# First attention layer: ScalarE instead of VectorE copies the linear logits, one place behind the newest piece

## What is computed

```python
xl = (x @ Wl).reshape(n_nodes, heads, ch)
xr = (x @ Wr).reshape(n_nodes, heads, ch)
m = xl[src] + xr[dst]
e = leaky_relu(m, 0.2)
logits = einsum('ehc,hc->eh', e, att)
ex = exp(logits - segment_max(logits, dst)[dst])
alpha = ex / segment_sum(ex, dst)[dst]
out = segment_sum(alpha[:, :, None] * xl[src], dst)
```

## Time and profile before

| | us |
|---|---|
| median of 3 runs | 4667.72 |
| lowest, highest | 4667.09, 4673.2 |
| the profiled execution | 4674.29 |
| its span | 4672.5 |
| PE, DVE, ACT, POOL busy in the span | 3182.7, 3001.3, 1859.1, 3206.7 |
| DVE, ACT busy from 2400 to 3380 us (980 us) | 948.1, 883.9 |

### The profile page before, as it was taken

How to read it: one execution, slowest core, us unless ns; L and a number is a source line. 1 busy time by engine, 2 the same in 40 slices (tenths; PEclk the granted TensorE clock), 3 DMA queues, 4 the chain that set the end, 5 groups by cost and what they waited for, 6 DMA issues and landing times. The chain is left out here.

```text
span 4672.5 us, 94838 instructions
## 1 busy us (share of the span) xinstructions
PE 3182.7 (68%) x15556; PEld 2384.7 (51%) x15557; DVE 3001.3 (64%) x8993; ACT 1859.1 (40%) x6063; POOL 3206.7 (69%) x3436
## 2 busy tenths in 40 slices
PE   4666666666556566565678777777765888888882
PEld 3544444445344444443356666666533666666662
DVE  6545455454333333333689999999955887787776
ACT  3222222223000000000469899998842444444444
POOL 4777777775777777776177777777525777777772
PEclk7788888888777877877889999999987999999996
DMA  4666666665333333334377777777624877887874
GB/s 149 194 190 191 191 191 191 191 192 151 109 105 104 104 104 104 104 104 104 96 202 232 228 225 224 228 226 224 187 76 135 231 223 225 225 228 223 229 222 123
DMA packets 469973, 816.08 MB, mean 175 GB/s; under 512 B 86369, under 2 KB 271578, under 8 KB 469786
## 3 DMA queue, kind: packets, MB, share of 16 engines
q0 software_dynamic: 156464, 429.23, 33.9%
q1 hardware_dynamic: 246010, 294.61, 21.0%
q10 hardware_dynamic: 67312, 90.51, 5.4%
HBM read 640.60 MB, written 173.40 MB: 174 GB/s over the span
## 5 line engine op out<-in xcount | busy, mean ns | idle before, releaser
L1009 POOL DMA_INDIRECT rows<-table_d,idx x3224 | 3068.9, 952 | 997.2 <-issue 918.1
L1185 PE MATMUL psum<-rows,selw 128*128 x3648 | 1206.7, 491 | 803.4 <-POOLq L1025 720.0
L1185 PEld LDWEIGHTS psum<-rows,selw 128*128 128x128 f32 x3648 | 855.0, 245 | 1080.7 <-issue 935.5
L2065 ACT ACTIVATE px<-rows,px 128x64 f32 (+1 forms) x4480 | 1265.9, 367 | 105.5 <-ACT px L2056 101.9
L2130 PE MATMUL psum<-px,ohf 128*128 128x264 f32 (+1 forms) x3648 | 949.5, 405 | 66.4 <-ACT px L2065 63.1
L1157 DVE TENSOR_TENSOR acc<-acc,psum 125x256 f32 x456 | 191.3, 419 | 1013.2 <-PE psum L1185 1012.6
L2130 PEld LDWEIGHTS psum<-px,ohf 128*128 128x128 f32 x3648 | 678.4, 196 | 202.5 <-issue 45.3
L2081 PE MATMUL psum<-xr,ohT 125*128 x5472 | 706.6, 281 | 60.3 <-DMA ohT<-ohT_d 35.0
L1897 DVE TENSOR_TENSOR m<-rows,psum 128x1024 f32<-128x1024 f32 x456 | 553.8, 1214 | 236.4 <-POOLq L1025 150.3
L2081 PEld LDWEIGHTS psum<-xr,ohT 125*128 125x128 bf16 x5472 | 541.9, 100 | 201.8 <-issue 75.1
L1146 DVE TENSOR_SCALAR selw<-iotaw,dst_t,w_t 128x128 f32 x1824 | 517.7, 359 | 180.5 <-issue 126.4
(11 more groups left out here) (319 smaller groups left out, 2038.2 us busy)
## 6 DMA issues: line engine op xcount, KB each, us to landing
ohf<-oh_d SPq DMA_DIRECT2D x456, 256.0 KB
oh_d<-ohfk ACTq DMA_DIRECT2D x228, 256.0 KB, 2.8
ohT<-ohT_d SPq DMA_DIRECT2D x456, 128.0 KB
rows<-table_d,idx POOLq DMA_INDIRECT x3224, 2.7
part_d<-part SPq DMA_DIRECT2D x228, 132.0 KB
part_d<-part SPq DMA_DIRECT2D x228, 129.0 KB
ohT_d<-ohTk ACTq DMA_DIRECT2D x228, 128.0 KB
flg<-flags_d SPq DMA_DIRECT2D x228, 40.0 KB
```

Source lines behind the costliest of these rows:

```text
L1009: pool.indirect_dma_start(out=rows[0:n, s % RING, k, :], out_offset=None, in_=table, in_offset=bass.IndirectOffsetOnAxis(ap=idx[0:n, s // ...
L1185: last = nc.tensor.matmul(ps[g.pos % DEEP], sel[:, g.pos % DEEP, k, :], rows[:, bass.ds(r, 1), k, :].squeeze(1), start=k == 0, stop=k == K ...
L2065: last = nc.scalar.activation(px[:, i, k, h, 0:C], rows[:, bass.ds(r, 1), k, h * C:(h + 1) * C].squeeze(1), ACT.Copy, scale=px[:, i, k, h, ...
```

## The change

In the first attention layer (H > 1) `linear` leaves VectorE's list. ScalarE gets a stage `linear_logits` with lag 1, between `exps` and `take`. It waits for the block's landing by itself, copies the same numbers into the same place and counts the same semaphore. The second layer (H == 1) keeps VectorE's stage.

```diff
                                   (1, scale), *([(1, reduce)] if H > 1 else []), (2, take_ends), (0, add), (5, factor_line), (3, pick),
-                                  (0, linear), (3, before), (1, scan), (12, bring), (2, join), (3, after),
+                                  *([(0, linear)] if H == 1 else []), (3, before), (1, scan), (12, bring), (2, join), (3, after),
@@
-                    packed_pieces(act, mybir.EngineType.Activation, blocks3, 3, 10, (10, probs), (10, weigh), (3, exps), (4, take))
+
+                    def linear_logits(g):
+                        if g.place == 0:
+                            wait(act, s_turned, g.chunks(2))
+                        b, r = block_of(g), ring_of(g)
+                        wait_alone(act, s_landed, b + 1)
+                        nc.scalar.copy(lin[:, g.half, g.place], rows[:, bass.ds(r, 1), :, D:D + H].squeeze(1)).then_inc(s_lin, 1)
+                    packed_pieces(act, mybir.EngineType.Activation, blocks3, 3, 10, (10, probs), (10, weigh), (3, exps),
+                                  *([(1, linear_logits)] if H > 1 else []), (4, take))
```

## The result

| | before | after |
|---|---|---|
| median of 4 runs, us | 4668.55 | 4893.12 |
| lowest, highest | 4667.09, 4673.2 | 4891.27, 4895.1 |
| span of the profiled execution | 4672.5 | 4891.0 |
| first to last scan of the layer | 1033.0 | 1254.0 |
| mean from scan to scan | 27.92 | 33.89 |

The ratio is 1.0478 (95% interval 1.0466 to 1.0491): 225 us slower, against the 212 of the prediction (4880, range 4815 to 4930). All of it lies in the first attention layer: first to last scan grew by 221 us. In the second layer the last scan comes at 4787.6 instead of 4569.1, 218.5 us later, the difference of the spans.

A forecast was written before the change was run, and what follows sets the result against it. VectorE and ScalarE both full, coupled by the chunk's chain. 35 x (33.94 - 27.92) = 211, with the end periods 217 us on 4674.3: 4891, median 4885, stated as 4880; range 4815 to 4930.

The forecast's parts named there:

- The closed loop: First attention layer: scan, VectorE, exps, four ScalarE steps, linear copy, turn_logits, scan; 33.94 us per chunk against 27.92.
- the turn: TensorE's turn_logits must wait for ScalarE's linear copies; lin to scan 0.83 us at full clock, 1.31 at half.
- VectorE's leg: VectorE from scan to fac: 11.87 us less two copies, plus 1.0 us of wait for spread_xr at half clock.
- ScalarE's leg without a turn: ScalarE from exps to the fourth weighing's end, 17.97 us, plus 0.7 for four copies and the last one's completion.
- The loop turn: ScalarE's stand where its own loop repeats: 2.09 us, in every second chunk.
- The clock: TensorE, idling longer, falls to half clock: lin to scan 1.31 us instead of 0.83, and VectorE waits 1.0 for spread_xr.
- VectorE's stands: VectorE standing 5 to 7 us before every scan, and busy near 79% in the layer.
- The first and last period: First chunk period, with three weighings, about +2 us; last, with one weighing of half length, about +4.
- Rival 3: No closed loop: ScalarE slides ahead once, then only its own work counts, 28.5 us per chunk; 4695 us, chance 0.04.
- Rival 4: Faster: VectorE ends the layer and ScalarE's gaps take the copies; 18 us less, 4650 us, chance 0.04.
- stands that keep the full clock: Some TensorE stands may keep full clock, one chunk in ten costing 5 us; forecast lowered from 4885 to 4880.

The follow-up runs named there:

- the wait alone: VectorE keeps its linear copy, ScalarE makes the same one into a spare tile, and turn_logits on TensorE also waits for it; 4897.93 us, 1.0472 to the kernel before.
- the two places of 1 us: Changed kernel plus eight ScalarE copies of 128x32 per chunk: between exps and turn_logits 4929.52 us; behind the chunk's last linear copy 4895.52 us.
- lag 0: Changed kernel with ScalarE's linear copy made for the newest piece, at the same place in the step; 4705.34 us, 1.0067 to the kernel before.
- fillers: Changed kernel with 21 unread 128x128 matmuls on TensorE ahead of the waits in turn_logits; 4874.15 us, 1.0439 to the kernel before.
- the spare copy: Kernel before, with ScalarE also making the linear copy into a spare tile that nobody waits for; 4711.97 us, 1.0073 to the kernel before.
- the slow batch: Third batch, kernel before at 5728.29 us; the kernel whose trace is cited is the kernel before plus 7 unread TensorE matmuls before the logits wait, 5773.64 us.

## Why the prediction was right

- The closed loop: right. Exps 0.03 us behind fac, four weighings, the copy, the turn, the scan, as walked above; shown by the wait alone, by the two places of 1 us, and by lag 0.
- VectorE's leg, scan to fac: 11.87 and 1.0 for the clock in the prediction, 12.87 in sum; measured 12.61 (13.03 behind even scans, 12.21 behind odd ones).
- ScalarE's leg without a turn: 18.67 predicted, 18.62 to the copy's end measured. A copy holds the engine for 0.10 us (2967.24 to 2967.34), not 0.15: the lower end. The page of the Trainium skill on ScalarE had it (ScalarE: Activation LUTs, What ACT_TABLE_LOAD costs; the estimate from it was 0.106), and the trace agrees. Four copies are 0.2 us shorter by it, and the weighings and what lies between them took 0.15 more than in the row that I had read.
- The loop turn: mis-sized. 2.09 us from before, 52.7 / 17 = 3.1 after. The periods with a turn are 36.1 us where 35.0 was expected (33.94 and half of the 2.09), the others 32.1 where 32.9 was. I took the turn from a program that the change makes longer.
- The clock: right in kind, too large. 1.48 us per chunk was predicted, 1.0 in VectorE's leg and 0.48 between copy and scan. Measured against the full-clock terms, VectorE's leg is 0.74 longer (12.61 against 11.87; but I had read two short legs, 12.03, where the mean of the trace before is 12.4, so part of this is not the clock's), and from the copy's end to the scan it is 1.42 instead of 0.83. Of these last 0.59 the turn itself (1.17 from its start to the scan) makes about 0.35; the rest is a hand-over from the copy's end to the turn of 0.39 us in the periods with a loop turn and 0.10 in the others, for which the runs show no cause. With fillers 19 us came back, 0.5 us per chunk. TensorE stood 5.6 and, with a loop turn, 8.2 to 9.6 us, where 5.3 and 7.4 were predicted. I had aggregate and `spread_xr` both slow in each chunk. That holds only behind the 5.6 us stands (3.73, and 1.8 to 2.3 us); behind the longer ones the aggregate took 3.0 to 3.7 us and `spread_xr` its usual 1.48, and VectorE hardly stood. The granted clock fell to 0.87, not 0.8. The Trainium skill (TensorE: Matmul & The Clock Gate, Part 1) has the throttled state as the default, which activity releases; the trace agrees, with 0.87 when TensorE stood and 0.96 when fillers kept it busy.
- VectorE's stands: 6.0 us per scan (222.1 in 37), inside the 5 to 7 on average, though 4.6 and 7.8 in turn. ScalarE's: 4.8 + 0.5 us per chunk, as expected near 5. VectorE busy 78%.
- The first and last period: 30.9 and 30.6 us, 3.0 and 3.5 more than before; 2 and 4 were predicted.
- Rival 3, the copy's own cost without the loop, was priced at 22 us; the spare copy cost 35, with the longer loop turn beside it again. Rival 4 was wrong at every place tried: with lag 0 the copy is off VectorE and the scan hardly waits for it, and it is still 28 us slower. So VectorE's 97% did not bound alone.

The terms of the loop, us, means of the 35 middle periods:

| | predicted | measured |
|---|---|---|
| scan to fac | 12.87 | 12.61 |
| fac to exps | 0.04 | 0.03 |
| exps to the last copy's end | 19.72 | 20.01 |
| copy's end to scan | 1.31 | 1.42 |
| period | 33.94 | 34.07 |

So the mechanism and the sizes hold, but that the period fits within 0.13 us is in part luck: VectorE's leg was 0.26 too long, ScalarE's 0.29 too short. The total would have been 4885 against 4893, had I not taken off 5 us for stands that keep the full clock; in the trace every turn of the logits from 2400 to 3600 us took 0.93 us to the aggregate's start, against 0.48 with the clock kept by fillers.

## What to carry to other kernels

When work moves to another engine, look up whose step its result must now wait for, and follow that engine back to what holds it; if that path returns to the waiting engine, add up the loop, since it, and no busy share, gives the period. A lag of one in a list of stages can be worth a whole step of the slower engine: here one digit decided 4.1% of the time, some 190 us. An engine's loop turn and the clock of an engine that is made to stand belong in the sum, and neither is the same after the change as before.

## What the hardware showed that was not expected

- A turn of ScalarE's loop of 12 pieces took 2.1 us before and 3.1 to 3.2 with one short stage more. Together with that came 17 to 19 more packets of instructions, and in the traces a second packet in the last 5.5 us of nearly every turn. VectorE's own loop turn shows no stand in the list of waits.
- A longer stand of TensorE did not cost more: behind 5.6 us the aggregate and `spread_xr` took 3.73 and 1.8 to 2.3 us, behind 8.2 to 9.6 us 3.0 to 3.7 and 1.48 us.
- Moving a copy that holds the engine for about 0.27 us per chunk from ScalarE to VectorE cost 28 us in all, with more than four times as many slow aggregates (32 against 7). That the clock makes the loss is argued, not shown.
- The kernel before took 4670 us in one batch and 5728 in another, under the same chip number. In the trace of a kernel of the slow batch VectorE's wide operations kept their durations (1.22 us for reduce), and its busy time over the whole program was 3008 us against 3001; TensorE's granted clock was 0.80 against 0.86.
